# An attention, batch norm, convolution and whitening chain: pairs 1, 2 and 8 with fp32 scores on the same rows, last shift by VectorE, two stores

## The reference, cut to what matters

```python
# x: (8, 64, 16, 16) fp32; layer 0, then layer 1, with N = 256, Cq = 8
xf = x.reshape(B, C, N)
q = jnp.einsum('oc,bcn->bno', Wq, xf) + bq
k = jnp.einsum('oc,bcn->bon', Wk, xf) + bk[:, None]
v = jnp.einsum('oc,bcn->bon', Wv, xf) + bv[:, None]
attn = jax.nn.softmax(jnp.einsum('bno,bom->bnm', q, k), axis=-1)
out = jnp.einsum('bcj,bij->bci', v, attn)        # layer 0: then Wo, bo, times gamma
x = x + out
...
# then: batch norm, relu, 3x3 convolution with one-bit weights, twice, plus x;
# then: per channel group a 4x4 covariance, its Cholesky factor, a solve and a 4x4 weight
```

## Time and profile before

| | |
|---|---|
| runs | 66.2, 65.73, 65.8 us; median 65.8 |
| the profiled execution | 65.95 us, of it 64.2 us span |
| mean granted TensorE clock | 0.989 |
| TensorE busy | 55.8 us (87% of the span), 803 matmuls |
| VectorE busy | 47.0 us (73%) |
| ScalarE busy | 41.8 us (65%) |
| GpSimd busy | 21.5 us (34%) |

### The profile page before, as it was taken

How to read it: one execution, slowest core, us unless ns; L and a number is a source line. 1 busy time by engine, 2 the same in 40 slices (tenths; PEclk the granted TensorE clock), 3 DMA queues, 4 the chain that set the end, 5 groups by cost and what they waited for, 6 DMA issues and landing times.

```text
span 64.2 us, 2136 instructions
## 1 busy us (share of the span) xinstructions
PE 55.8 (87%) x803; PEld 34.7 (54%) x803; DVE 47.0 (73%) x124; ACT 41.8 (65%) x135; POOL 21.5 (34%) x64
## 2 busy tenths in 40 slices
PE   5997999499997995995999897999899999999900
PEld 2345454275653623441655564689776997955500
DVE  0069998698958888498895888899479978577630
ACT  0713289999997797979979196690039563278830
POOL 5000683830645508258212107317303050025000
PEclk9999999999999999999999999999999999999995
DMA  0888881000000000000000000000000000000054
GB/s 0 216 232 199 282 303 51 0 0 10 0 0 0 0 5 0 10 0 5 0 5 0 0 0 0 10 0 10 0 0 0 10 0 10 0 0 0 0 167 160
DMA packets 2457, 2.71 MB, mean 42 GB/s; under 512 B 400, under 2 KB 2064, under 8 KB 2448
## 3 DMA queue, kind: packets, MB, share of 16 engines
q1 hardware_dynamic: 2016, 2.26, 11.8%
q10 hardware_dynamic: 432, 0.33, 1.5%
HBM read 2.06 MB, written 0.52 MB: 40 GB/s over the span
## 4 chain that ended last, share of the span: by engine, by line
PE 63%; DVE 19%; issue 7%; POOL 3%; ACT 2%; DVEq 0%; POOLq 0%; ACTq 0%
PE bank L942 12%; PE bank L717 12%; PE both L834 10%; PE bank L757 4%; DVE negmax L1083 3%; DVE cut L1095 3%; PE both L728 3%; PE bank L800 2%; DVE x L1135 2%; PE bank L775 2%; DVE qk L1112 2%; PE bank L792 2%; PE both L918 2%; PE bank L978 2%; PE bank L742 2%
## 5 line engine op out<-in xcount | busy, mean ns | idle before, releaser
L562 ACT ACTIVATE probs<-bank 128x512 f32<-128x512 f32 x16 | 8.6, 586 | 1.4 <-PE bank L800 1.3
L717 PE MATMUL bank<-const-bfloat16-1.0 128*64 128x512 bf16 x60 | 8.7, 433 | 0.8 <-PEq L1390 0.8
L542 ACT ACTIVATE bank<-bank,negmax 128x256 f32<-128x256 f32 x20 | 9.0, 453 | 0.6 <-DVE negmax L1083 0.4
L834 PE MATMUL both<-probs,vt 128*64 128x256 f32 x56 | 7.7, 390 | 0.0
L1083 DVE TENSOR_REDUCE negmax<-bank 128x2 f32<-128x512 f32 x10 | 6.7, 686 | 1.0 <-PE bank L775 0.6
L542 ACT ACTIVATE both<-both,negmax 128x256 f32<-128x256 f32 x12 | 5.4, 447 | 1.6 <-DVE negmax L1083 1.6
L369 POOL TENSOR_TENSOR cut<-cut 64x256 f32<-64x256 f32 x7 | 4.3, 611 | 6.2 <-DVE cut L1095 5.4
L942 PE MATMUL bank<-hi,taps 64*64 64x225 f16 (+2 forms) x126 | 5.9, 267 | 0.1
L942 PE MATMUL bank<-lo,taps 64*64 64x225 f16 (+2 forms) x126 | 5.9, 265 | 0.0
L385 POOL TENSOR_TENSOR shift<-negmax,lntot 128x4 f32<-128x4 f32 x8 | 1.6, 202 | 12.2 <-issue 11.8
L717 PEld LDWEIGHTS bank<-const-bfloat16-1.0 128*64 128x64 bf16 x60 | 3.5, 120 | 3.5 <-issue 1.6
(11 more groups left out here) (163 smaller groups left out, 121.9 us busy)
## 6 DMA issues: line engine op xcount, KB each, us to landing
cw<-conv_w SPq DMA_DIRECT2D x2, 288.0 KB, 4.8
x<-x_in SPq DMA_DIRECT2D x4, 128.0 KB, 3.0
kst<-consts SPq DMA_DIRECT2D x1, 428.0 KB, 5.9
out<-res SPq DMA_DIRECT2D x3, 128.0 KB, 1.9
aw<-attn_w ACTq DMA_DIRECT2D x1, 128.0 KB, 2.5
aw<-attn_w SPq DMA_DIRECT2D x1, 128.0 KB, 3.6
out<-res ACTq DMA_DIRECT2D x1, 128.0 KB, 1.8
half<-select SPq DMA_DIRECT2D x1, 96.0 KB, 3.1
```

The lines of the kernel that those rows point to most:

```text
L542: nc.scalar.activation(part, part, ACT.Exp, bias=negmax[:, i % 2, n:n + 1], accum_out=total[:, i % 2, n:n + 1]).then_inc(total_out, 1)
L562: nc.scalar.activation(probs[:, i % 2, g], pb_t[g][:].rearrange("p (t n) -> p t n", t=CH), ACT.Exp).then_inc(exp_out, 1)
L717: mm(bank[lanes(h)], filler[:, lanes(h)], filled, start=True, stop=True)
L834: last = mm(mixed(i)[g * C:(g + 1) * C], vt[:, i % 2, t, g * C:(g + 1) * C], probs[:, i % 2, g, t, :], start=(t == 0 and i < ITERS - 1), s ...
```

## The change

1. `DIRECT = (0, 1, 7)`: for pairs 1, 2 and 8 the scores are made in fp32. `project` writes four column strips of 32 with a shifted slice of the weights each, so that queries of image `g` come to rows `32g` and keys to rows `64 + 32g` of another bank. `direct_queries` (VectorE) and `direct_keys` (ScalarE) add the bias and put both on rows 0 to 63 of `fp_qk`; there is no splitting, no `replicate` and no `queries_keys` for these pairs. `direct_scores` and `scores_t` multiply 8 rows of fp32 per image. For pairs 2 and 8 `direct_scores` is called for each image by itself. The semaphores that count the split pairs go by `splits(i)`.
2. `value_weights` comes later on TensorE and, with `value_bias`, later on ScalarE. The two `keep_warm` calls in the front are gone. Tile 3 of `x` is loaded ahead of the selectors.
3. `shift_rows(3)` and `shift_rows(4)` come behind the first image's sums of the next pair; `totals(7, 0)` comes before `exps(5)`, `totals(7, 1)` behind it. `shifts_to_rows(3)` comes before `values(3)`, `shifts_to_rows(5)` writes to the bank `pb_rep`.
4. The last `shifts` is `last_shifts` on VectorE. `values(6)` comes behind `add_shifts(6)`, `values(7)` behind `add_shifts(7)`.
5. `signs(0)` comes before `exps(7)`; `magnitudes(0)` on ScalarE takes the place of `weight_sum(0)`; `weight_sum(1)` comes behind `statistics(2)`.
6. Two stores of 256 columns by 2, both by SP, in place of four.

```diff
--- before.py
+++ after.py
...
+DIRECT = (0, 1, 7)
...
-WARM_START = (6, 3, 4)
+WARM_START = 6
...
         def rows_of(i):
 
-            return pb_s[(2 * i + 1) % 3][:, 0:N]
+            return (pb_rep if i == 5 else pb_s[(2 * i + 1) % 3])[:, 0:N]
...
+            return (pb_v if i == 3 else pb_pv)[:, N:2 * N]
+
+        def direct_banks(i):
+
+            return {0: (pb_pv[:, N:2 * N], pb_s[1][:, 0:N]), 1: (banks[7][:, N:2 * N], pb_s[2][:, 0:N]),
+                    7: (pb_pv[:, N:2 * N], pb_v[:, N:2 * N])}[i]
+
+        def direct_bias(i, o):
+
+            return prm[lanes(o), P_DIRECT + i // PAIRS:P_DIRECT + i // PAIRS + 1]
+
...
-
-                sp.wait_ge(res_act, n + 1)
-                sp.wait_ge(res_dve, n + 1)
-                sp.dma_start(out[:, quarter(n)], res[:, quarter(n)]).then_inc(stored, 16)
-            sp.wait_ge(stored, 16 * len(PIECES))
+            for n in range(2):
+
+                sp.wait_ge(res_act, 2 * n + 2)
+                sp.wait_ge(res_dve, 2 * n + 2)
+                both_pieces = slice(2 * n * N, 2 * n * N + 2 * N)
+                sp.dma_start(out[:, both_pieces], res[:, both_pieces]).then_inc(stored, 16)
+            sp.wait_ge(stored, 32)
...
                                      ACT.Identity).then_inc(v_out, 1)
 
+            def direct_keys(i):
+
+                act.wait_ge(proj_mm, i + 1)
+                nc.scalar.activation(fp_qk[:, DIRECT.index(i), 1], direct_banks(i)[1][lanes(1)], ACT.Identity,
+                                     bias=direct_bias(i, 1)).then_inc(keys_out, 1)
...
 
             first_bias()
+            direct_keys(0)
+            direct_keys(1)
+            totals(0, 0)
             value_weights()
             value_bias()
-            act.wait_ge(rep_mm, 1)
-            nc.scalar.activation(qk[:, 0, 1], pb_s[2][:, 0:N], ACT.Identity).then_inc(k0_out, 1)
-            totals(0, 0)
             totals(0, 1)
             logs(0)
-            first_values()
             totals(1, 0)
             totals(1, 1)
...
             totals(2, 0)
             totals(2, 1)
@@ -592,27 +614,30 @@
             totals(3, 1)
             logs(3)
             exps(2)
+            totals(4, 0)
             shift_rows(3)
-            totals(4, 0)
             totals(4, 1)
             logs(4)
             exps(3)
+            totals(5, 0)
             shift_rows(4)
-            totals(5, 0)
             totals(5, 1)
             logs(5)
-            exps(4)
+            exps(4, (0,))
+            direct_keys(7)
+            exps(4, (1,))
             totals(6, 0)
             totals(6, 1)
             logs(6)
+            totals(7, 0)
             exps(5)
-            totals(7, 0)
             totals(7, 1)
             logs(7)
             exps(6)
+            signs(0)
             exps(7)
-            signs(0)
             signs(1)
+            magnitudes(0)
 
             act.wait_ge(last_stats, 1)
             nc.scalar.activation(xs[LAYERS][:, quarter(PAIRS - 1)], mixed(ITERS - 1), ACT.Identity).then_inc(x_last, 1)
...
+                if i in DIRECT:
+                    for r in range(P // BLOCK):
+                        first = w + r * CQ
+                        to = slice(r * BLOCK, (r + 1) * BLOCK)
+                        last = mm(direct_banks(i)[r // G][to], aw[:, first:first + BLOCK], x_of(i), start=True, stop=True)
+                else:
+                    for h in range(2):
+                        last = mm(proj(i)[lanes(h)], aw[:, w + h * C:w + (h + 1) * C], x_of(i), start=True, stop=True)
                 last.then_inc(proj_mm, 1)
 
             def replicate(i):
...
                 last.then_inc(v_mm, 1)
 
+            def direct_scores(i, images):
+
+                pe.wait_ge(part0_out, i + 1)
+                pe.wait_ge(keys_out, DIRECT.index(i) + 1)
+                for g in images:
+                    if 2 * i + g >= 3:
+                        pe.wait_ge(total_out, CH * (2 * i + g - 2))
+                q, k = (fp_qk[:, DIRECT.index(i), o] for o in range(2))
+                for t in range(CH):
+                    for g in images:
+                        rows = slice(BLOCK * g, BLOCK * g + CQ)
+                        last = mm(pb_s[(2 * i + g) % 3][:, t * N:(t + 1) * N], q[rows, t * P:(t + 1) * P], k[rows],
+                                  start=True, stop=True)
+                        if t == CH - 1:
+                            last.then_inc(s_mm, 1)
...
                     for g in range(G):
+                        if i in DIRECT:
+                            q, k = (fp_qk[BLOCK * g:BLOCK * g + CQ, DIRECT.index(i), o] for o in range(2))
+                            mm(pb_t[g][:, t * N:(t + 1) * N], k[:, t * P:(t + 1) * P], q, start=(t == 0), stop=False,
+                               skip_group_check=True)
+                            continue
                         rows = slice(C * g, C * (g + 1))
...
                 pe.wait_ge(shift_out, i + 1)
+                if i == 5:
+                    pe.wait_ge(qk_out, splits(ITERS))
...
                 last.then_inc(pv_mm, 1)
 
-            keep_warm(WARM_START[0], pb_t[0])
+            keep_warm(WARM_START, pb_t[0])
 
             project(0)
+            project(1)
+            direct_scores(0, range(G))
+            project(2)
             value_weights()
-            project(1)
-            replicate(0)
-            project(2)
-            scores(0)
+            direct_scores(1, (0,))
+            direct_scores(1, (1,))
             scores_t(0)
             project(3)
-            replicate(1)
+            replicate(2)
             values(0)
-            pe.wait_ge(part0_out, 3)
-            keep_warm(WARM_START[1], pb_pv)
-            scores(1)
-            replicate(2)
-            keep_warm(WARM_START[2], pb_pv)
             shifts_to_rows(0)
...
             replicate(4)
             project(5)
             scores(4)
+            shifts_to_rows(3)
             values(3)
-            shifts_to_rows(3)
             scores_t(3)
             mix(2)
             replicate(5)
...
             add_shifts(4)
             project(7)
             scores(6)
+            shifts_to_rows(5)
+            direct_scores(7, (0,))
             values(4)
-            shifts_to_rows(5)
+            direct_scores(7, (1,))
             scores_t(5)
-            replicate(7)
             add_shifts(5)
+            last_shortcut()
             values(5)
-            scores(7)
             mix(4)
             shifts_to_rows(6)
             scores_t(6)
-            last_shortcut()
+            add_shifts(6)
             values(6)
-            add_shifts(6)
             mix(5)
-            values(7)
             shifts_to_rows(7)
             scores_t(7)
             add_shifts(7)
+            values(7)
             mix(6)
             mix(7)
 
...
-                ve.tensor_tensor(some, some, tops(some), ALU.subtract).then_inc(part2_out, 1)
+            def direct_queries(i):
+
+                dve.wait_ge(proj_mm, i + 1)
+                ve.tensor_scalar(fp_qk[:, DIRECT.index(i), 0], direct_banks(i)[0][lanes(0)],
+                                 direct_bias(i, 0), None, ALU.add).then_inc(part0_out, 1)
 
...
                                pb_v[:, 0:CH * P].rearrange("p (t c) -> p t c", t=CH)).then_inc(v_out, 1)
+
+            def last_shifts():
+
+                i = ITERS - 1
+                dve.wait_ge(ln_out, ITERS)
+                dve.wait_ge(rows_mm, i - 1)
+                ve.tensor_tensor(shifts_of(i, 0), negmax[:, i % 2].rearrange("p (g u) -> p g u", g=G),
+                                 lntot[:, i % 2].rearrange("p (g u) -> p g u", g=G),
+                                 ALU.subtract).then_inc(shift0_out, 1)
+                dve.wait_ge(shift0_out, ITERS)
+                ve.tensor_tensor(shifts_of(i, 1), shifts_of(i, 0), shift_tops(i, 0),
+                                 ALU.subtract).then_inc(shift1_out, 1)
+                dve.wait_ge(shift1_out, ITERS)
+                ve.tensor_tensor(shifts_of(i, 2), shifts_of(i, 1), shift_tops(i, 1),
+                                 ALU.subtract).then_inc(shift_out, 1)
 
             def shift_rows(i):
 
@@ -1147,17 +1199,14 @@
 
 
             powers_of_two()
-            first_parts(0)
-            later_parts(0)
-            first_parts(1)
-            queries_keys(0)
+            direct_queries(0)
+            direct_queries(1)
+            maxima(0, 0)
             first_parts(2)
-            maxima(0, 0)
             maxima(0, 1)
-            queries_keys(1)
-            first_parts(3)
             maxima(1, 0)
             maxima(1, 1)
+            first_parts(3)
             queries_keys(2)
             shift_rows(0)
             maxima(2, 0)
@@ -1183,27 +1232,26 @@
             maxima(5, 1)
             add_shortcut(3)
             queries_keys(6)
-            first_parts(7)
+            direct_queries(7)
             maxima(6, 0)
             maxima(6, 1)
+            shift_rows(5)
+            maxima(7, 0)
             values_out(4)
```

(9 more changed lines are left out.)

85 lines of the change are left out of this document (35 added, 50 removed).

## The result

The changed kernel takes 77.83 us (median of four runs, 76.42 to 81.05) against 65.92 us for the kernel before in the same session: 1.181 times as long; over the executions that the ratio counts it is 1.166, with a 95% interval of 1.152 to 1.180. The direction was as predicted. The size was not: 68.2 us was forecast, and 69.0 was the upper end of the range. The traced execution took 77.34 us with a span of 75.6. Some executions, those of the kernel before among them, take about 1.5 us longer than the others (in the traced one of b_last_shift, 67.2 us, TensorE's clock rose only at about 9.3 us, before at 4.8), so ratios leave them out (here 76.42 and 77.34 us count), and where a ratio is not given the lowest times are compared.

A forecast was written before the change was run, and what follows sets the result against it. TensorE, with 63% of the chain, was taken to set the end after ScalarE's early pace. Terms 0.38 + 0.46 + 0.88 + 0.81 = +2.53 us, trimmed to +2.4 on a 65.8 median, gave 68.2 us, range 67.4 to 69.0.

The forecast's parts named there:

- The rival: Front: a 0.4 us gap before the second input delays TensorE's clock rise; up to 71.0 us, chance 0.08.
- Its 256 columns stream as in `mix`: Price of an fp32 score product with 8 rows in a 32-row strip: 0.43 us a round, as in `mix`.
- `project(3)` ends for VectorE at 10.8, so `first_parts(3)` runs to 11.25: Front, VectorE: `queries_keys(2)` then runs to 11.85, so the first shift copy starts at 11.85 us, as before.
- the 0.96 us at the start: Front, pair 1: ScalarE's first sum starts at 7.29 us instead of 8.25, spent again before pair 1's exponentials.
- The fp32 block: Direct scores on TensorE: two rounds take 0.85 us, 0.96 with one change of tiling mode.
- the term that the prediction had no row for: TensorE: three drains between 32-row and 64-row strips at 0.11 us; counting them at half takes about 0.15 off.
- The bound of 1.2 us: Upper bound for an fp32 score block, if weights could not be loaded ahead.
- all three terms: Tail from `shifts_to_rows(5)` to `mix(7)`: +0.46 to `add_shifts(6)`, +0.88 to `shifts_to_rows(7)`, +0.81 to `mix(7)`.
- the 0.88 us: Tail: TensorE waits for the last shift, queued on VectorE behind `values_out(6)` and `statistics(0)`; +0.88 us.
- The two stores at 0: End: two 256 KB stores for four of 128 KB cost 0, bounds -0.2 and +0.4 us.
- ScalarE keeps the pace alone: Rival: TensorE's longer blocks fall into its gaps, so ScalarE's savings give 64.9 us; chance 0.1.
- the two effects cancel: Rival: the change makes no difference, 65.8 us; chance 0.06.

The follow-up runs named there:

- b_last_shift: Kernel before with the last shift as three VectorE operations behind `statistics(0)` in place of GpSimd's: 65.95 us, ratio 1.0005.
- a_fill_wait: Changed kernel with four filler calls of 128-row bf16 products in TensorE's wait for the second pair's input: 81.34 us.
- m_rows: Kernel before with fp32 products over 8, 8+8, 32, 64 and 32+32 rows appended, alternating with 128-row stages: 157.34 us.
- c_values0: a_rows64 with `scores_t(0)` moved behind `project(3)`, `replicate(2)` and `values(0)` on TensorE: 70.44 us, ratio 1.069 to the kernel before.
- a_rows64: Changed kernel with queries and keys on 64 rows per image, 56 of them zero, and wider projections: 71.03 us, ratio 1.080 to the kernel before.
- a_rows32: Changed kernel with fp32 scores over all 32 rows of each strip instead of 8, scores not the reference's: 81.28 us.
- x_front_only: Kernel before with only the change's front (pairs 1 and 2 direct, changed loads and early order) and two stores: lowest 71.92 us.
- c_values6: a_rows64 with `values(6)` ahead of `add_shifts(6)` on TensorE: 70.5 us, ratio 1.070 to the kernel before.
- b_stores: Kernel before with two stores of 256 KB for four of 128 KB: lowest 65.79 us, against 65.60 before.
- m_mix: Kernel before with appended fp32 stages: 32-column weights, mixes of 8-row and 128-row products, six and twelve 8-row products alone: 160.15 us.
- c_pair1: Kernel before with pair 1 alone scored directly in fp32 over 8 rows, and two stores: 66.15, 69.3, 69.63 and 71.66 us.

## Why the prediction failed, point by point

| From one point to the next, us | before | predicted | changed kernel | 64 rows (clock 1.00) |
|---|---|---|---|---|
| to `shifts_to_rows(5)` | 28.54 | +0.38 | +7.18 | +2.58 |
| to `add_shifts(6)` | 5.44 | +0.46 | +2.28 | +0.66 |
| to `shifts_to_rows(7)` | 1.67 | +0.88 | +0.88 | +0.88 |
| to `mix(7)` | 2.04 | +0.81 | +0.93 | +0.82 |
| sum | | +2.53 | +11.27 | +4.94 |

**The clock, some 6.2 us (11.27 - 4.94, less 0.11 in the last row, where both ran at full clock).** This step failed most: the sum has every block at full clock. The rival was there, with a chance of 0.08 and 71.0 us as its end. Its mechanism, a rise put off by a gap ahead of the second input, is refuted by the trace of the changed kernel, where the clock rose at about 5.0 us in spite of the gap, and by a_fill_wait. What the runs showed in its place is a fall under work, behind products over few rows, with the gap and without it. Its price was sized as the new products at half speed. In truth the fall lasted 13.6 and 3.4 us, beyond the products that set it off, and each product in it, `mix` above all, took about twice as long. The prediction's sentence "Its 256 columns stream as in `mix`" is right as to the length of a product and leaves out what it does to the next ones. The Trainium skill (TensorE: Matmul & The Clock Gate, Part 1) tells of an idle TensorE that is throttled and of activity that releases the clock. The traces show something else beside it: TensorE without a gap, busy for 4.00 us of 4.00, at 1.2 GHz under 8-row products in m_rows.

**The front, 2.58 instead of 0.38.** The step "`project(3)` ends for VectorE at 10.8, so `first_parts(3)` runs to 11.25" failed. `first_parts(3)` waits for `values(0)` as well as for `project(3)`, because both use one bank. In the changed kernel `values(0)` stands behind `replicate(2)`, so VectorE stood still for 3.43 us (15.44), and for 1.50 with the clock at 1.00. The shift copy came at 16.44, and at 13.88 with 64 rows, not at 11.85. c_values0 gives 0.64 us of it back. The prediction took the end of a product as the end of the wait, without looking at what else the waiting operation asks for.

This wait is the smaller part of the 2.2 us beyond the prediction. In a_rows64 `shifts_to_rows(0)` starts at 12.59 us instead of 11.27, 1.3 late, and the shift copy at 13.88 instead of 11.85, 2.0 late: TensorE itself is 1.3 us late, and 0.7 is the wait. No run takes the 1.3 apart, but the trace does. The second input let `project(1)` start at 5.61 us in the changed kernel and at 5.48 in a_rows64 instead of 4.97; in a_rows32 and x_front_only, with the loads of the changed kernel, it was 4.95 and 4.86, so this differs from execution to execution. The wider projection of a_rows64, 1.01 us for 0.57, is its own and not the change's. And `direct_scores(0)` took 1.07 us (6.49 to 7.56), where the prediction's timeline of the front gave it 0.86 (5.5 to 6.36), less than its own price of 0.96. These three make 1.2 us. The first sum came at 8.07 us rather than 7.3, so that only 0.18 of the 0.96 us at the start were won. From 5.48 us to 12.87 TensorE has no wait in a_rows64: it sets the front there.

**The fp32 block, 1.06 instead of 0.96.** Between two starts inside a block there are 0.21 us, behind the first 0.32, and from the last to the next block 0.31 (6.18, 6.50, 6.72, 6.93, 7.24 in the changed kernel, of which the first row is shown). So there are two steps that are 0.1 longer, where the prediction counted one. The one at the end is a change of tiles. The block of `scores_t(7)` shows what the new strips of 32 rows do to it: in front of `add_shifts(7)`, which has strips of 64 rows, it takes 1.07 us with strips of 32 (46.22 to 47.29) and 0.97 with strips of 64 in a_rows64 (40.00 to 40.97). That is the term that the prediction had no row for, 0.11 for each change between strips of 32 and of 64 rows: it was right to count it. The Trainium skill (TensorEngine Tiling, Key Properties) puts the drain at a change of mode; the trace agrees, with 0.1 us at this change. In front of the column tiles of a projection the strips of 64 pay it as well (6.49 to 7.56). The long step behind the first product is what the prediction missed. It is there with strips of 32 and of 64 rows, and no run shows its cause; the bf16 `scores(1)` of the kernel before goes in from column tiles too and has 0.12 us there (9.62 to 9.74). The bound of 1.2 us held.

**The tail.** At full clock all three terms came out: 6.10 against 5.90 us, 2.55 against 2.55, and 2.86 against 2.85. In the changed kernel the stretch from `shifts_to_rows(5)` to `last_shortcut` is still at full clock and takes 3.49 us (35.72 to 39.21) against 3.26 in the prediction's sum, for two blocks that are each 0.1 longer. The last step is 2.97 us there and 2.86 in a_rows64, which is the 0.1 of `scores_t(7)` above. c_values6 shows that some 0.6 of the 0.88 us had the reason given. b_last_shift shows that without the queue ahead of it the move costs nothing.

**The end.** The two stores at 0 stand as far as b_stores can tell. The span from the start of `mix(7)` to the end of the span is 26.6 us in the changed kernel and 26.5 before.

**The other rivals.** "ScalarE keeps the pace alone" and "the two effects cancel" are refuted by a_rows64, which at full clock is 8% slower. Without the clock the time would have been near 71.0 us, or 70.6 without what a_rows64's wider projection adds (an estimate, from its 1.01 us for 0.57), at least 1.6 beyond the upper end: even then the range was too narrow, because the front's neutral balance rested on one overlooked wait and on durations taken at their lower side.

No kernel here beats the one before. Of those with fp32 scores the nearest, pair 1 alone, came within 0.3% of it once (66.15 us against 65.96) and was slower by 5% and more in three of four runs.

## What to carry to other kernels

A product over few rows of the array isn't only as long as one over all rows; a group of them can also halve TensorE's clock for several microseconds after it, with TensorE busy all the time. What held the clock in every run here was to fill the rows with zeros up to 64 per image (a_rows64 and the two kernels built on it, ten executions); look first at what the wider projection costs. Mixing such products with others is less sure: four and four over 128 rows held it in m_mix, but in c_pair1 a single block among other work was followed by a fall in some runs. Compare the duration of one known block before you trust the recorded clock. And when a step is moved ahead, read every semaphore that its consumer waits for, and the bank that it shares: the wait that was hidden is the one that sets the time next.

## What was not expected of the hardware

- The granted clock falls to 1.2 GHz under products over 8 rows or 32 rows that leave no gap, also when two 8-row products run side by side; it holds at 2.4 GHz under 64 rows, under two times 32 side by side, and under 128 rows with only 32 columns of weights (m_rows, m_mix).
- Six fp32 products over 8 rows, 2.8 us, between long stretches over 128 rows were followed by a fall. It came at about 133.8 us, after they had ended, and lasted some 3.4 us. Four at a time (1.9 us), alternating with four over 128 rows, were not (m_mix); in c_pair1 one block of 1.06 us was in some runs and not in others. The clock can also come back during such products: in the changed kernel at about 22.1 us, in a block over 8 rows (21.31 to 22.73).
- The record of the granted clock said 1.00 in the front of a_rows32, up to about 27 us, while the products there took 0.63 us instead of 0.37.
- An fp32 block over strips of 32 rows is 0.1 us longer than one over strips of 64 rows when strips of 64 follow (1.07 and 0.97 us).
- The same load of the second input, issued at 1.63 us, held TensorE up until 5.61 us in the traced execution of the changed kernel, 4.95 in a_rows32 and 4.86 in x_front_only, which have the same loads in the same order. A fixed landing time for an early load is no safe term of a sum.
